# Dividing attention's sums of heads with dims on partitions, in another order of groups

## What is computed

```python
def _L1_attn_ref(x, Wq, Wk, Wv, Wo):
    ...
    att = jnp.einsum('bhtd,bhsd->bhts', q, k) / jnp.sqrt(jnp.asarray(hd, x.dtype))
    att = att + mask
    w = jax.nn.softmax(att, axis=-1)
    z = jnp.einsum('bhts,bhsd->bhtd', w, v)
    z = z.transpose(0, 2, 1, 3).reshape(B, T, D)
    return z @ Wo.T
...
x = x + _L0_attn_ref(_layernorm(x, axis=-1), ...)
x = x + _L0_ffn_ref(_layernorm(x, axis=-1), ...)
x = x + _L1_attn_ref(_layernorm(x, axis=-1), ...)
x = x + _L1_ffn_ref(_layernorm(x, axis=-1), ...)
```

## Time and profile before

| what | us |
|---|---|
| median of 3 runs | 439.1 |
| lowest and highest run | 437.48, 444.05 |
| span of the profiled execution, first to last instruction | 441.7 |
| PE busy | 410.0 (93%) |
| DVE busy | 297.1 (67%) |
| ACT busy | 232.9 (53%) |
| POOL busy | 170.2 (39%) |

### The profile page before, as it was taken

One profiled execution on the slowest core, in us unless ns is written; L12 is line 12 of the kernel. 1 busy time (PEld: TensorE's weight loads), 2 busy tenths in 40 slices (PEclk: granted clock), 3 DMA queues, 4 the chain that ended last, 5 costly groups with the idle time before them and its releaser, 6 DMA issues.

```text
span 441.7 us, 14528 instructions
## 1 busy us (share of the span) xinstructions
PE 410.0 (93%) x6328; PEld 237.2 (54%) x6328; DVE 297.1 (67%) x596; ACT 232.9 (53%) x377; POOL 170.2 (39%) x250
## 2 busy tenths in 40 slices
PE   5799789999999988999999998998999999888997
PEld 5356564555555347544377466544555553465476
DVE  4636489999998216521336586899999981188883
ACT  3535355577776973221101541655877769635950
POOL 4107013314033144478692000234361544453770
PEclk9989799999999999999999997999999999999999
DMA  6899550000000000200100479400000000000002
GB/s 204 129 239 263 128 148 4 4 3 4 4 2 5 4 1 6 65 8 9 64 0 0 120 200 224 106 5 4 3 4 3 4 5 2 2 1 0 1 26 71
DMA packets 21657, 22.97 MB, mean 52 GB/s; under 512 B 2588, under 2 KB 20858, under 8 KB 21594
## 3 DMA queue, kind: packets, MB, share of 16 engines
q1 hardware_dynamic: 20498, 19.03, 17.8%
q0 software_dynamic: 544, 2.49, 1.9%
q10 hardware_dynamic: 552, 0.53, 0.4%
HBM read 8.27 MB, written 1.05 MB: 21 GB/s over the span
## 4 chain that ended last, share of the span: by engine, by line
PE 71%; DVE 14%; ACT 4%; DMA 3%; issue 3%; POOL 2%; SPq 2%; ACTq 0%; DVEq 0%
PE ps L785 11%; PE ps L765 11%; DVE mx L1258 11%; PE ps L743 10%; PE ps L916 8%; PE ps L1012 5%; PE ps L944 4%; PE ps L921 4%; ACT prob L1141 4%; PE ps L677 4%; PE ps L980 4%; DMA col_rows<-in_L_ffn_up_scale 3%; PE ps L845 3%; PE ps L751 2%; POOL xn L605 1%
## 5 line engine op out<-in xcount | busy, mean ns | idle before, releaser
L1258 DVE TENSOR_REDUCE mx<-ps 128x1 f32<-128x512 f32 (+3 forms) x304 | 181.1, 654 | 28.9 <-PE ps L751 24.1
L1141 ACT ACTIVATE prob<-ps 128x1024 f32<-128x1024 f32 (+1 forms) x192 | 145.4, 812 | 63.4 <-PE ps L765 63.1
L743 PE MATMUL ps<-kS,qS 96*32 96x512 bf16 (+21 forms) x1536 | 111.9, 321 | 4.4 <-DVE mx L1258 3.0
L590 POOL TENSOR_SCALAR_AFFINE_SELECT prob<-prob 128x256 f32<-128x256 f32 x128 | 51.9, 412 | 163.9 <-ACT prob L1141 162.5
L765 PE MATMUL ps<-qS,kS 101*32 101x512 bf16 (+7 forms) x1536 | 95.2, 326 | 3.7 <-ACT prob L1141 3.6
L785 PE MATMUL ps<-prob,v 128*32 128x512 f32 (+3 forms) x768 | 80.1, 489 | 0.6 <-POOL prob L590 0.4
L743 PEld LDWEIGHTS ps<-kS,qS 99*32 99x32 bf16 (+1 forms) x1536 | 42.8, 95 | 50.4 <-DVE mx L1258 28.1
L748 PE MATMUL ps<-mask_q,identb 128*32 128x32 bf16 (+1 forms) x1024 | 51.1, 186 | 2.7 <-issue 2.7
L765 PEld LDWEIGHTS ps<-qS,kS 101*32 101x32 bf16 (+1 forms) x1536 | 35.0, 96 | 31.2 <-ACT prob L1141 15.8
L751 PE MATMUL ps<-mask_q,identb 128*32 128x64 bf16 (+1 forms) x512 | 45.4, 198 | 0.0
L748 PEld LDWEIGHTS ps<-mask_q,identb 128*32 128x32 bf16 x1024 | 28.1, 98 | 14.0 <-issue 9.2
(11 more groups left out here) (146 smaller groups left out, 537.0 us busy)
## 6 DMA issues: line engine op xcount, KB each, us to landing
qS<-parts SPq DMA_DIRECT2D x24, 128.0 KB, 3.3
kS<-parts SPq DMA_DIRECT2D x24, 128.0 KB, 3.4
qS<-prob SPq DMA_DIRECT2D x12, 128.0 KB, 8.0
kS<-prob SPq DMA_DIRECT2D x12, 128.0 KB, 7.5
qS<-xn SPq DMA_DIRECT2D x12, 128.0 KB, 3.4
kS<-xn SPq DMA_DIRECT2D x12, 128.0 KB, 2.9
out<-x SPq DMA_DIRECT2D x8, 128.0 KB, 1.7
oT<-in_L_ffn_gate_w POOLq DMA_DIRECT2D x1, 768.0 KB, 4.8
```

The source lines that it names most:

```text
L590: nc.gpsimd.affine_select(out=square, in_=square, compare_op=ALU.is_ge, fill=0.0, base=0, pattern=[[0, 2], [1, P]], channel_multiplier=-1) ...
L743: mmi = nc.tensor.matmul(span[r:r + STRIP, 0:seen], qS[0:K_MAX[L], c, g * G + h, qt * P + r:qt * P + r + STRIP], kS[0:K_MAX[L], g * G + h, ...
L1141: nc.scalar.activation(prob[:, n % 3, 2 * pair:2 * pair + 2, off:CH], ps[:, 2 * (m % 2):2 * (m % 2) + 2, off:CH], ACT.Exp, scale=SCALE).th ...
L1258: ins = nc.vector.tensor_reduce(mx[:, slot, qt, heads[0]:heads[-1] + 1, part], src, AX_X, ALU.max)
```

## The change

The columns of ones in `v1` are now interleaved with the values, so that in each head's rows sums and denominators alternate. When ACT has copied a group's product into `oT`, SP moves the even partitions to `num` (in the place of `xnT`) and the odd ones to `den` (in the place of `xn`), two DMAs a group (`move_o`). Both then have dims on partitions: 128 rows for half of the heads (`j`), 512 columns for a chunk. DVE divides there (`divide`): a reciprocal of `den` in place, and a multiply into `num`, in six pieces a layer, two of 512 columns and four of 256 (`NORMS_EARLY` four, `NORMS_LATE` two). Wo multiplies directly from `num`, in pairs of tiles (`WO_PAIRS`): tiles 4, 5 within step 1 of the last group, 6, 7 within its step 3 (`WO_WITHIN`), tiles 0, 1 and 2, 3 ahead of the FFN's hidden tiles 2 and 3 (`WO_BEHIND`). The transposes to queries and back, `onT`, ACT's copies into it and the early jobs are gone.

The order of groups is new: chunk 0 of groups 0 and 1, chunk 1 of all four, chunk 0 of groups 2 and 3. DVE normalises all tiles, POOL none. The transposes of chunk 0 stand ahead of hidden tile 4 (layer 0) and 5 (layer 1). The first rounding step of DVE moves from hidden tile 2 to 4 of chunk 1, the second from 2 to 3 of chunk 0; POOL loads the weights as soon as the moves have landed, and computes the last rstd behind that. The two halves of `xnT` that layer 1's FFN reads lie by chunk now.

```diff
-TURNS_BEHIND = (2, 3)
+TURNS_BEHIND = (4, 5)
...
+WO_PAIRS = ((4, 5), (6, 7), (0, 1), (2, 3))
+WO_BEHIND = {2: (0, 1), 3: (2, 3)}
+WO_WITHIN = {1: (4, 5), 3: (6, 7)}
...
+ROUND_AT = ((0, 4), (1, 3))
...
+WIDE = 256
+NORMS_EARLY = [(0, 0, 0, CH), (0, 1, 0, CH), (1, 1, 0, WIDE), (1, 1, WIDE, CH)]
+NORMS_LATE = [(1, 0, 0, WIDE), (1, 0, WIDE, CH)]
+N_NORM = len(NORMS_EARLY) + len(NORMS_LATE)
...
+def norms_for(pair):
+
+    j, c, first, end = (NORMS_EARLY + NORMS_LATE)[-4 + WO_PAIRS.index(pair)]
+    assert (j, c, first) == (CJ - 1, pair[0] // TPC, pair[0] % TPC * P)
+    return len(NORMS_EARLY) - 2 + WO_PAIRS.index(pair) + 1
...
-CGS = [(0, 0), (1, 0), (2, 0), (0, 1), (1, 1), (2, 1), (3, 1), (3, 0)]
+CGS = [(0, 0), (1, 0), (0, 1), (1, 1), (2, 1), (3, 1), (2, 0), (3, 0)]
...
+        if s - last in WO_WITHIN:
+            order.append(("wo", WO_WITHIN[s - last]))
...
+        num = xnT
+        den = xn[:, :, :].rearrange("p t i -> p (t i)").rearrange("p (c j q) -> p c j q", c=NC, j=CJ)
...
-        onT = sb("onT", [P, 2, CJ, P], F32)
-        rec = sb("rec", [P, 2, NH], F32)
...
+        def o_landed(L):
+
+            return 16 * 2 * (L + 1) * NG // CJ
...
+            def move_o(L, cg):
+
+                g, c = CGS[cg]
+                j, half = g * CJ // NG, slice(g % (NG // CJ) * G * HD, (g % (NG // CJ) + 1) * G * HD)
+                sp.wait_ge(o_taken, L * N_CG + cg + 1)
+                for part, dst in enumerate((num[half, j, c * CH:(c + 1) * CH], den[half, c, j, :])):
+                    sp.dma_start(dst, oT[part:P:2, g, c * CH:(c + 1) * CH]).then_inc(o_moved[j][c], 16)
...
+                    if cg == 1:
+                        sp.wait_ge(a_full, A_AT["v", L, NT - 1] + 1)
+                        for k in range(N_QK):
+                            sp.wait_ge(stacked[k], 16 * len(Q_PARTS) * (L + 1))
+                    move_o(L, cg - 1)
+                move_o(L, N_CG - 1)
...
-            nc.gpsimd.memset(v1[:, :, :, HD:2 * HD], 1.0).then_inc(ones_v, 1)
+            nc.gpsimd.memset(v1[:, :, :, 1::2], 1.0).then_inc(ones_v, 1)
...
-                    if n // 2 % 2 and first >= TPC:
-                        pool.wait_ge(rstd_done, pair + 1)
-                        for t in (first, first + 1):
-                            nc.gpsimd.tensor_scalar(xn[:, t], x[:, t], mv[:, t, 0:1], rstd[:, t:t + 1],
-                                                    ALU.subtract, ALU.mult).then_inc(xn_pool, 1)
...
-            rstd_of(3)
-
-            pool.wait_ge(ffn1s_in, 16)
-            pool.wait_ge(b_full, B_AT["wo", 0, RING[-1]] + 1)
             w8_src = [a["L1_ffn_gate_w"].rearrange("(j p) i -> p j i", p=P),
                       a["L1_ffn_up_w"].rearrange("(j p) i -> p j i", p=P),
                       a["L1_ffn_down_w"].rearrange("(k p) i -> p k i", p=P)]
             for n in range(2):
-                if n:
+                if n == 0:
+                    for j in range(CJ):
+                        for c in range(NC):
+                            pool.wait_ge(o_moved[j][c], o_landed(0))
+                else:
                     pool.wait_ge(w8_round, n)
                 pool.dma_start(w8.rearrange("p (j i) -> p j i", j=w8_src[n].shape[1]), w8_src[n]).then_inc(w8_in, 16)
+                if n == 0:
+                    rstd_of(3)
...
-                        early_jobs(L, entry[1])
...
-            def query_major(bank, t):
...
-            def dim_major(bank, t):
...
-            def times_wo(L, bank, t):
...
-            def early_jobs(L, kind):
...
-            def behind_early(L, job):
...
-                        query_major(bank, t).then_inc(b_full, 1)
...
-                        dim_major(bank, t).then_inc(a_full, 1)
...
-                        times_wo(L, bank, t).then_inc(b_full, 1)
...
+                        pe.wait_ge(m_free, (L + 1) * N_MAX)
+                        times_wo(L, entry[1])
+
+            def times_wo(L, pair):
+
+                bank = take_b(("wo", L, pair))
+                pe.wait_ge(o_normal, L * N_NORM + norms_for(pair))
+                for n, t in enumerate(pair):
+                    for j in range(CJ):
+                        mmi = nc.tensor.matmul(bank[:, n * C:(n + 1) * C], num[:, j, t * P:(t + 1) * P], attn_w(L, 3)[:, j, :],
+                                               start=j == 0, stop=j == CJ - 1)
+                mmi.then_inc(b_full, 1)
+                pe.wait_ge(s_free, 2 * (L + 1) * N_STEP)
+                pe.wait_ge(o_taken, (L + 1) * N_CG)
+                ln_transposes("ffnT", 2 * L + 1, FFN_C[0], L, *((take_a, a_full) if L == 0 else (take_b, b_full)))
...
+                        if c == FFN_C[0] and ht in WO_BEHIND:
+                            times_wo(L, WO_BEHIND[ht])
...
-                    nc.scalar.copy(v1[:, t, :, 0:HD], bank[:, 0:C].rearrange("p (h d) -> p h d", h=NH)).then_inc(a_free, 1)
+                    nc.scalar.copy(v1[:, t, :, 0::2], bank[:, 0:C].rearrange("p (h d) -> p h d", h=NH)).then_inc(a_free, 1)
...
-                for n, t in enumerate(RING):
-                    if n == len(RING) - 1:
-                        transposed_half(FFN_C[0])
-                    bank = bank_a(("onT", L, t))
-                    if n >= 2:
-                        act.wait_ge(b_full, B_AT["wo", L, RING[n - 2]] + 1)
-                    else:
-                        act.wait_ge(e_full, e_made(L, "wo"))
-                    nc.scalar.copy(onT[:, t % 2].rearrange("p j q -> p (j q)"), bank[:, 0:C]).then_inc(a_free, 1)
-                    if n == 0:
-                        nc.scalar.activation(warm[:], nhalf[:, 0:1], ACT.Silu)
+                nc.scalar.activation(warm[:], nhalf[:, 0:1], ACT.Silu)
+                transposed_half(FFN_C[0])
...
-                def divide(bank, t):
-
-                    bank = bank.rearrange("p (h d) -> p h d", h=NH)
-                    chain(nc.vector.reciprocal(rec[:, t % 2].unsqueeze(2), bank[:, :, HD:HD + 1]))
+                def divide(norm):
+
+                    j, c, first, end = norm
+                    dve.wait_ge(o_moved[j][c], o_landed(L))
+                    below, above = den[:, c, j, first:end], num[:, j, c * CH + first:c * CH + end]
+                    chain(nc.vector.reciprocal(below, below))
-                    return nc.vector.tensor_tensor(xn[:, t].rearrange("p (h d) -> p h d", h=NH), bank[:, :, 0:HD],
-                                                   rec[:, t % 2].unsqueeze(2).to_broadcast([P, NH, HD]), ALU.mult)
+                    nc.vector.tensor_tensor(above, above, below, ALU.mult).then_inc(o_normal, 1)
+
+                def add_wo(pair):
+
+                    bank = bank_b(("wo", L, pair))
+                    tiles = slice(pair[0], pair[-1] + 1)
+                    nc.vector.tensor_tensor(x[:, tiles], bank.rearrange("p (t i) -> p t i", t=len(pair)), x[:, tiles],
+                                            ALU.add).then_inc(b_free, 1)
+                    dve.wait_ge(b_free, B_AT["wo", L, pair] + 1)
+                    for t in pair:
+                        ln_stats(t)
...
-                for kind in E_JOBS:
...
-                    if kind == "on":
-                        chain(nc.vector.reciprocal(rec[:, :].unsqueeze(3), heads[:, :, :, HD:HD + 1]))
-                for n in range(len(RING) + 2):
-                        divide(bank_b(("on", L, RING[n])), RING[n]).then_inc(b_free, 1)
-                        add_to_x("wo", L, t).then_inc(b_free, 1)
-                        if L == 0 and ht == 2:
-                            ln_normalise(2 * L + 1, FFN_C[1])
...
+                for norm in NORMS_EARLY:
+                    divide(norm)
+                for pair in WO_PAIRS[0:2]:
+                    add_wo(pair)
+                ln_normalise(2 * L + 1, DVE_TILES[1][0:TPC])
+                if L == 1:
+                    transposed_half(FFN_C[0])
+                for norm in NORMS_LATE:
+                    divide(norm)
+                        if L == 0 and (i, ht) in ROUND_AT:
+                        if i == 0 and ht in WO_BEHIND:
+                            add_wo(WO_BEHIND[ht])
...
+                        if i == 0 and ht in WO_BEHIND:
+                            ln_normalise(2 * L + 1, WO_BEHIND[ht])
```

## The result

The changed kernel takes 459.0 us (median of 4 runs, 457.6 to 461.6) against 438.3 for the kernel before (median of 4): ratio 1.048, 95% interval 1.042 to 1.054. It is slower, by 20.7 us, where 10.9 were forecast (450.0, range 436 to 460).

A forecast was written before the change was run, and what follows sets the result against it. DVE bounds early attention, PE the middle, and a serial 13.3 us tail ends each layer. Median 439.1 + 5.8 (layer 0 +1.9, layer 1 +3.9) + 5.1 for clock falls = 450.0 us, range 436 to 460.

The forecast's parts named there:

- The order of groups (+0.6): Attention, each layer: DVE-bound start -7.0 us, extra maxima +1.1, one more four-step group without maxima +6.5; sum +0.6.
- The order costs more: Rival: maxima cost all of 2.75 us, extra group late behind moves; some +3 a layer, 456; chance 0.15 with late moves.
- The division: DVE: reciprocals of 4.34 us (512 wide) and 2.22 (256), each with a multiply of 0.69 or 0.42.
- The rival of a cheap reciprocal: Long contiguous reciprocals run like a plain pass, under about 2.5 us for 512: no stalls, 434.0 us; chance 0.13.
- Behind the stall: From the first Wo pair to the FFN: attention ends at 173.4 instead of 168.03, FFN starts 3.7 us earlier.
- FFN, layer 0 (+5.6): Layer 0's FFN: two Wo pairs +4.0 us, normalising tiles 2, 3 +1.1, tiles waiting for late rstd +0.5.
- FFN, layer 1 (+7.1): Layer 1's FFN: two Wo pairs +4.0 us, PE's wait by hidden tile 5 +3.1; DVE's low halves +0.5 besides.
- the 16.6 us in that sum: DVE's work before layer 1's chunk-0 transposes end at hidden tile 5, against 12.7 us of PE: PE waits 3.9.
- The moves on SP (0): Sixteen 128 KB moves a layer between maximum transfers: hidden, the last transfer covered by 0.5 us; cost 0.
- The clock (+5.1): Clock falls to 1.2 GHz behind three waits of 3.9 us, 1.7 us each; +5.1 in all.
- the two stalls at the first Wo pair: Last attention group, each layer: PE waits 3.9 us for three divisions ending at 166.4 before Wo of tiles 4, 5.
- the prediction's gap of 4.3: Layer 0, from the end of PE's attention, forecast at 173.4, to the FFN's start, forecast at 177.7.

The follow-up runs named there:

- the mask: Changed kernel with DVE's mask of layer 1's down weights one group earlier (third group's turn, not fourth): 448.3 us, ratio 1.026 to the kernel before.
- the run with filled waits: Changed kernel with that mask one group earlier, plus unread 512-column products in PE's waits for normalised tiles: 444.5 us, ratio 1.016.
- the Wo pairs earlier: Against the run with filled waits, the last two Wo pairs of each layer one hidden tile earlier: 444.1 us, ratio 1.013.
- POOL held back: Against the Wo pairs earlier, POOL's first subtraction in layer 1's FFN waits until DVE has normalised the last tiles: 442.5 us, ratio 1.005.
- the best form of the new scheme: Against POOL held back, the second early Wo pair behind step 2, not 3, with fewer filling products: 440.4 us, ratio 1.004.
- the last run: Against the best form of the new scheme, all products that fill waits removed: 442.8 us, ratio 1.013.

## Why the prediction was right in sign and short in size

**The order of groups (+0.6)** is the step that failed. As work of DVE and PE it was well sized: 1.0 us a layer. But the step followed these two engines alone. It looked at POOL's queue in the gap and in the FFN, not in attention, and so missed that a constant which counts places in the list of groups stayed at 3 while the list under it changed. The missing term is 10.8 us by the stages and 10.7 by the medians, or 9.8 with each median taken against the kernel before beside it: as much as the 9.8 by which the change cost more (20.7) than forecast (10.9). "The order costs more" stood among the rivals, at 456, with all of the extra maxima's work and a last transfer late behind the moves as its mechanism. That mechanism did not occur: apart from the mask the order costs 1.0 a layer and not 3, and PE's waits for a maximum's transfer come to 0.2 us in the whole changed kernel. The range reached up to 460 for the sake of that rival, so it is by luck that 459.0 lies inside it.

**The division** was over-sized. The reciprocal of 512 took 3.35 us, not 4.34, that of 256 1.75, not 2.22. DVE's timeline in layer 0, then PE at the first Wo pair:

```profile
148.00 3.35 DVE L1282 RECIPROCAL xn<-xn 128x512 f32<-128x512 f32 x1
151.39 0.94 DVE L1284 TENSOR_TENSOR xnT<-xnT,xn 128x512 f32<-128x512 f32 x1
152.25 3.34 DVE L1282 RECIPROCAL xn<-xn 128x512 f32<-128x512 f32 x1
...
156.23 1.75 DVE L1282 RECIPROCAL xn<-xn 128x256 f32<-128x256 f32 x1
158.01 0.42 DVE L1284 TENSOR_TENSOR xnT<-xnT,xn 128x256 f32<-128x256 f32 x1
```

```profile
158.58 1.97 PE L850 MATMUL ps<-w,xnT 128*128 128x256 f32 x8 [0.88 <-DVE xnT L1284]
```

Between 256 and 512 an element costs (3.35 - 1.75) us / 256, some 6.3 ns, not the 8.3 of the widths 16 and 32 in the earlier trace rows. Three divisions take 10.4 us instead of 12.8, and PE waits 0.88 us (0.89 in layer 1) where 3.9 were forecast, with the releaser that was named. Not all of that is the reciprocal: counted from layer 0's first score, the third division ends 1.9 us earlier than forecast, and PE comes to the pair 1.3 us later. No fall follows that short wait. The Trainium skill ("VectorE: DVE Perf Modes", First, the fixed hardware budget) speaks of a repeat count of 8, which gave 4.27 us as an estimate; the measured 3.35 is a fifth under it. The rival of a cheap reciprocal needed less than 2.5 us and is out. The multiply that the prediction let meet POOL's triangles takes 0.94 us at 151.39, beside them, and 0.69 the next time; the 0.25 is within the forecast's bound of one triangle (0.41).

**Behind the stall.** From the first score to the FFN's start layer 0 takes 118.1 instead of 122.8, 4.7 us less, where 3.7 were forecast: attention grew by 3.6 and not 5.4, since the stall was smaller, and the gap is 5.0, not 4.3. Of the 3.6 the order makes 1.0 and the reciprocals 1.1; what makes the other 1.5 was not taken apart.

**FFN, layer 0 (+5.6).** It grew by 7.3, with a fall of the clock at 168; without that fall, in the run with filled waits, by 5.1. There the forecast held, without counting a fall.

**FFN, layer 1 (+7.1).** It grew by 11.4, with two falls, and by 9.0 with one half fall left. The wait ahead of hidden tile 5 is there, 3.35 us against the 3.9 forecast (3.1 net of transposes), but for another reason than the sum of DVE's work: without the reciprocals, 4.4 of the 16.6 us in that sum (3.5 as measured), it stays. So the size came out by luck. It is the chain from the second pair's product, with the normalisations slowed by POOL; the second of PE's two waits is for a bank that DVE frees behind them. PE's timeline:

```profile
419.26 0.41 PE L702 MATMUL ps<-ident,xn 128*128 128x128 f32 x2 [1.38 <-DVE xn L1185]
421.65 0.69 PE L702 MATMUL ps<-ident,xn 128*128 128x128 f32 x2 [1.97 <-DVEq L1347]
```

**The moves on SP (0)** hid as forecast: the one visible wait for them is 0.45 us of DVE ahead of a late division, which nobody waits for.

**The clock (+5.1).** Of the three places forecast, behind the two stalls at the first Wo pair and behind the wait at tile 5, only the last came out. The other falls are behind the idle stretches of 2.04 us after attention, which the prediction's gap of 4.3 contained without asking for the idle time in it, and behind the stall that was not forecast. PE's timeline in layer 1's gap; layer 0's has the same 2.04:

```profile
399.85 0.91 PE L702 MATMUL ps<-ident,xn 128*128 128x128 f32 x4 [2.04 <-DVE xn L1185]
```

The size was not measured as a whole: filling the two gaps and a part of the wait at tile 5 gave 3.9 us back by the medians (4.1 in the two FFNs), and what the fall behind the stall costs is part of the mask's 10.8.

Step by step from the changed kernel to the kernel before, by the stages' sums: the mask 10.8; filling 1.5 (3.8 without the chance fall in layer 1's attention); the Wo pairs earlier 5.0 (2.7 without it); POOL held back 0.6; the second pair earlier 2.0; left 0.4. Together 20.3. The steps of 0.6 and 2.0 are no larger than the scatter of these sums. In the best form of the new scheme the two gaps together are 19.0 us shorter than before (7.6 against 26.6), and the two attentions and FFNs 18.7 longer (3.8, 4.2, 4.3 and 6.4): two late Wo pairs, 4.0, stand in each FFN, the order costs 1.0 a layer, and most of the rest is waits (PE idles 7.6 and 8.1 us in the two attentions against 4.6 and 5.0 before). Whether other places of the pairs would turn that into a gain was not tried.

## What to carry to other kernels

When a list of work is reordered, look for every constant that counts places in it and ask each in-order queue, not only the busiest two, what now stands ahead of the next needed instruction: here one index, through an engine that is busy 35% of the time, cost as much as all the rest of the change. A rate read from short instructions in one memory need not be the price of long ones in another (8.3 ns an element against 6.3 here). And a shorter tail is worth little if its work moves to stages that have no gap and leaves idle stretches behind that let the clock fall.

## What the runs showed of the hardware

DVE's normalisation (one instruction of 256 elements with two scalars, from SBUF to SBUF) slows with what POOL does: two took 0.73 us with POOL idle and 2.39 beside two POOL subtractions of 512, ending 0.15 us after these. The Trainium skill ("SBUF — State Buffer", Who interferes with whom) says that such an instruction, in a mode that takes both of its ports, and a GpSimd instruction shut each other out for a whole instruction; the rows agree with that, and none shows the mode.

The length of one idle stretch alone doesn't say whether the clock falls: 1.3 us of PE idle left it at 1.00 in the kernel before, and 1.89 us ahead of hidden tile 5 did so in the run with the Wo pairs earlier, while behind 1.23 us, followed by transposes with further short waits, it fell to 1.2 GHz in the last run (0.57 as the mean of the 4 us in the window). With products that nobody reads in the waits behind attention it stayed at 1.00.
